# A projection with a 64-row contraction: products of two token tiles in the two row halves of TensorE's array, and a row list read back one block later

## The reference, cut to what matters

```python
scores = jnp.einsum('bsd,d->bs', x, W[0]) + b[0]
_, top_idx = jax.lax.top_k(scores.reshape(B, n_blocks, 128), 16)
h = jnp.take_along_axis(x, sel_idx[:, :, None], axis=1)      # (8, 512, 128)
# retention, on a layer-normalised h
latent = jax.nn.silu(rmsnorm(h, ln_w) @ Wc)                  # 128 -> 64
q, k, v = jnp.split(latent @ Wqkv, 3, axis=-1)               # 64 -> 384
params = (latent @ Wreso).reshape(B, L, H, 4)                # 64 -> 16
gate_val = jax.nn.silu(latent @ Wg)                          # 64 -> 128
...
return out @ Wp * gate_val
```

## Time and profile before

| | |
|---|---|
| median of three runs | 2539.25 us (2531.22 to 2540.06) |
| the profiled execution's own time | 2540.07 us |
| its span, first to last instruction | 2537.9 us |
| busy: TensorE, its weight load, VectorE, ScalarE, GpSimd | 2184.6, 1531.1, 2010.7, 1757.8, 1551.5 us |
| granted TensorE clock, mean of the span | 0.91 |

### The profile page before, as it was taken

One profiled execution on the slowest core, in us unless ns is written; L12 is line 12 of the kernel. 1 busy time (PEld: TensorE's weight loads), 2 busy tenths in 40 slices (PEclk: granted clock), 3 DMA queues, 4 the chain that ended last, 5 costly groups with the idle time before them and its releaser, 6 DMA issues. The chain is left out here.

```text
span 2537.9 us, 48686 instructions
## 1 busy us (share of the span) xinstructions
PE 2184.6 (86%) x12375; PEld 1531.1 (60%) x12376; DVE 2010.7 (79%) x3333; ACT 1757.8 (69%) x5024; POOL 1551.5 (61%) x1693
## 2 busy tenths in 40 slices
PE   4558088683999999999999999999999999966993
PEld 2324066672666666666666666666666666666883
DVE  5943988314999999999999999999999999856664
ACT  2234253251888888888888888888888888823773
POOL 2642812372677777677777776677677767723773
PEclk9855587695999999999999999999999999976997
DMA  6410002351000000000000000000000000034555
GB/s 210 150 26 0 0 1 68 99 150 43 0 1 0 1 0 0 0 0 0 0 0 0 0 0 0 0 0 0 0 0 0 0 0 0 0 77 102 160 152 151
DMA packets 79707, 88.54 MB, mean 35 GB/s; under 512 B 22656, under 2 KB 56448, under 8 KB 77568
## 3 DMA queue, kind: packets, MB, share of 16 engines
q1 hardware_dynamic: 61184, 66.12, 9.3%
q0 software_dynamic: 8192, 16.87, 2.4%
q10 hardware_dynamic: 10240, 4.59, 0.7%
HBM read 73.87 MB, written 13.68 MB: 34 GB/s over the span
## 5 line engine op out<-in xcount | busy, mean ns | idle before, releaser
L1841 POOL TENSOR_TENSOR attend_weights<-attend_weights,attend_scales 128x512 f32<-128x512 f32 x1024 | 1048.5, 1047 | 474.8 <-DVE attend_scales L1757 474.8
L1735 DVE TENSOR_REDUCE attend_maxima<-attend_psL 128x16 fp32r<-128x1024 f32 x512 | 623.8, 1218 | 86.7 <-PE attend_psL L1657 86.7
L1751 DVE TENSOR_REDUCE attend_sums<-attend_weights 128x16 f32<-128x1024 f32 x512 | 618.5, 1208 | 4.1 <-ACT attend_weights L1787 4.1
L1801 ACT ACTIVATE attend_turned<-attend_psT 128x512 f32<-128x512 f32 x1024 | 556.6, 600 | 6.9 <-PE attend_psT L1676 6.6
L1676 PE MATMUL attend_psT<-consts,attend_weights 128*128 128x128 f32 x4096 | 530.4, 272 | 0.9 <-POOL attend_weights L1841 0.9
L1676 PEld LDWEIGHTS attend_psT<-consts,attend_weights 128*128 128x128 f32 x4096 | 477.1, 140 | 69.7 <-POOL attend_weights L1841 3.0
L1689 PE MATMUL attend_psA<-attend_turned,attend_chunk_values 128*64 128x512 f32 x2048 | 495.9, 605 | 0.8 <-ACT attend_turned L1801 0.8
L1795 ACT ACTIVATE attend_weights<-attend_psL,attend_maxima 128x64 f32<-128x64 f32 x2048 | 448.8, 334 | 52.0 <-DVE attend_maxima L1735 52.0
L1656 PE MATMUL attend_psL<-keys,attend_q_high 128*128 (+1 forms) x1024 | 434.2, 424 | 5.6 <-ACT attend_weights L1795 4.0
L1657 PE MATMUL attend_psL<-keys,attend_q_low 128*128 (+1 forms) x1024 | 404.2, 395 | 0.0
L1787 ACT ACTIVATE attend_weights<-attend_psL 128x512 f32<-128x512 f32 x512 | 316.1, 617 | 0.0
(11 more groups left out here) (318 smaller groups left out, 2565.6 us busy)
## 6 DMA issues: line engine op xcount, KB each, us to landing
moe2mix_w_tile<-in_L_ffn_w_dram SPq DMA_DIRECT2D x72, 256.0 KB
select_xbuf<-in_x_dram SPq DMA_DIRECT2D x16, 1024.0 KB, 4.9
moe1mix_w_tile<-in_L_ffn_W_dram SPq DMA_DIRECT2D x40, 256.0 KB, 2.7
select_emb<-L_attn_video_embeds_dram ACTq DMA_DIRECT2D x16, 256.0 KB, 3.1
moe2back_back<-result SPq DMA_DIRECT2D x8, 512.0 KB, 7.2
normed<-moe2route_normed SPq DMA_DIRECT2D x4, 520.0 KB, 9.2
normed<-moe1route_normed SPq DMA_DIRECT2D x4, 512.0 KB, 4.1
moe1back_back<-result SPq DMA_DIRECT2D x4, 512.0 KB, 5.9
```

What stands on the lines that cost most here:

```text
L1735: dve.tensor_reduce(maxima[:, both, :].rearrange("p j v -> p (j v)"), psL[:, both, :].rearrange("p j (v f) -> p (j v) f", f=FR), X, ALU.ma ...
L1751: dve.tensor_reduce(sums[:, both, :].rearrange("p j v -> p (j v)"), weights[:, both, :].rearrange("p j (v f) -> p (j v) f", f=FR), X, ALU. ...
L1801: act.activation(turned[:, parity, :, j * P:(j + 1) * P], psT[:, j % 2, :].rearrange("p (k q) -> p k q", k=SUB), ACT.Copy).then_inc(turned ...
L1841: pool.tensor_tensor(w, w, scales[:, s, :, None].to_broadcast([P, VC, FR]), ALU.mult).then_inc(normalised, 1)
```

## The change

The latents of tokens 0 to 255 of a batch are written to partitions 0 to 63, those of tokens 256 to 511 to partitions 64 to 127: two products of 256 columns, into the two partition halves of `psL`, in place of one of 512, and one silu on 128 partitions. `wall` is loaded a second time, to partitions 64 to 127, by ScalarE's queue. `project` now takes a pair of tiles, one in each row half, in the order q/k/v of half 0, q/k/v of half 1, gate of half 0, gate of half 1, each half with its own PSUM bank; a batch's tiles come in the order 0, 2, 1, 3. GpSimd's `square` therefore waits for the whole batch.

The second row list is written in the selection block but read back in the projection block, between SyncE's loads; GpSimd waits for it after its first two roots. Three small loads have a semaphore of their own (`first_in`), and `between(1)` waits for these alone; the decay rates are made one and two turns of the loop later. The last batch's squares are added up before the first gate step.

```diff
+def get_rows(sp, K, f):
+    part = slice(f * G // 2, (f + 1) * G // 2)
+    sp.wait_ge(K.rows_out, 16 * (f + 1))
+    sp.dma_start(K.rowidx[:, part], K.rows_dram.rearrange("(g p) -> p g", p=P)[:, part],
+                 allow_slow_non_contiguous=True).then_inc(K.rows_back, 16)
...
-        rows = sb("rows", [P, 2, TOP], U32)
+        rows = (sb("rows", [P, TOP], U32), K.last_rows)
...
                 put_rows(1)
-                get_rows(1)
...
-                pool.wait_ge(rows_back, 32)
...
-            wall = sb1("wall", [LAT, QKV + D])
+            wall = sb1("wall", [P, QKV + D])
-            latT = sb1("latT", [LAT, 2, L])
+            latT = sb1("latT", [P, 2, L // 2])
-            psL = ps1("psL", [LAT, L])
+            psL = ps1("psL", [P, 512])
-            psG = ps1("psG", [P, 2, TB, D])
+            psG = ps1("psG", [P, 2, 2, 512])
+            TILES = (0, 2, 1, 3)
+            def load_wall(engine, side):
+                part = slice(side * LAT, (side + 1) * LAT)
+                engine.dma_start(wall[part, 0:3 * D], a["L0_attn_Wqkv"]).then_inc(wall_in, 16)
+                engine.dma_start(wall[part, 3 * D:QKV], a["L0_attn_Wreso"]).then_inc(wall_in, 16)
+                engine.dma_start(wall[part, QKV:QKV + D], a["L0_attn_Wg"]).then_inc(wall_in, 16)
...
             def square(pool, b):
                 for g in range(b * TB, (b + 1) * TB):
-                    pool.wait_ge(qkv_copied, g + 3)
+                    pool.wait_ge(qkv_copied, b * TB + TB + 2)
...
                 def _(sp):
-                    sp.dma_start(wc[:], a["L0_attn_Wc"]).then_inc(s_const, 16)
-                    sp.dma_start(wall[:, 0:3 * D], a["L0_attn_Wqkv"]).then_inc(s_const, 16)
-                    sp.dma_start(wall[:, 3 * D:QKV], a["L0_attn_Wreso"]).then_inc(s_const, 16)
-                    sp.dma_start(wall[:, QKV:QKV + D], a["L0_attn_Wg"]).then_inc(s_const, 16)
+                    sp.dma_start(wc[:], a["L0_attn_Wc"]).then_inc(first_in, 16)
+                    sp.dma_start(lnw[:], column(a["L0_attn_ln_w"])).then_inc(first_in, 16)
+                    sp.dma_start(hd[:], everywhere(a["L0_attn_head_decay"], H0)).then_inc(first_in, 16)
+                    load_wall(sp, 0)
+                    get_rows(sp, K, 1)
                     sp.dma_start(wp[:], a["L0_attn_Wp"]).then_inc(s_const, 16)
-                    sp.dma_start(lnw[:], column(a["L0_attn_ln_w"])).then_inc(s_const, 16)
...
                     sp.dma_start(temp[:], everywhere(a["L0_attn_temperature"], 1)).then_inc(s_const, 16)
-                    sp.dma_start(hd[:], everywhere(a["L0_attn_head_decay"], H0)).then_inc(s_const, 16)
...
                     norm.roots(pool, K, 0, 2)
+                    pool.wait_ge(K.rows_back, 32)
...
                         if b == 1:
-                            dve.wait_ge(s_const, 16 * 11)
+                            dve.wait_ge(first_in, 48)
                             dve.tensor_scalar(wc[:], wc[:], lnw[:, 0:1], None, ALU.mult).then_inc(weights_ready, 1)
-                            dve.tensor_scalar(wp[:], wp[:], memw[:, 0:1], None, ALU.mult).then_inc(weights_ready, 1)
+                        if b == 2:
                             dve.wait_ge(act_decay, 1)
...
-                        if b == 2:
+                        if b == 3:
+                            dve.wait_ge(s_const, 16 * 5)
+                            dve.tensor_scalar(wp[:], wp[:], memw[:, 0:1], None, ALU.mult).then_inc(weights_ready, 1)
                             dve.wait_ge(act_decay, 3)
...
-                    for b in range(B - 3, B - 1):
+                    for b in range(B - 3, B):
                         sum_squares(b)
                     dve.wait_ge(act_gates, 1)
...
-                    sum_squares(B - 1)
...
+                    load_wall(act, 1)
...
                         act.wait_ge(s_latent, b + 1)
-                        act.activation(latT[:, s, :], psL[:], ACT.Silu).then_inc(latent_done, 1)
+                        act.activation(latT[:, s, :], psL[:, 0:L // 2], ACT.Silu).then_inc(latent_done, 1)
...
-                    act.wait_ge(weights_ready, 2)
+                    act.wait_ge(first_in, 48)
...
                         pe.wait_ge(latent_done, b + 1)
-                        pe.matmul(psL[:], wc[:], xnT[:], start=True, stop=True).then_inc(s_latent, 1)
+                        for side in range(2):
+                            mm = pe.matmul(psL[side * LAT:(side + 1) * LAT, 0:L // 2], wc[:], xnT[:, side * (L // 2):(side + 1) * (L // 2)],
+                                           start=True, stop=True, skip_group_check=True)
+                        mm.then_inc(s_latent, 1)
...
-                    def project(b, s, i):
+                    def project(b, s, pair):
...
-                        pe.wait_ge(qkv_copied, b * TB + i + 1)
-                        pe.matmul(psQ[:, i % 2, 0:QKV], lat, wall[:, 0:QKV], start=True, stop=True).then_inc(qkv_ready, 1)
-                        mm = pe.matmul(psG[:, s, i, :], lat, wall[:, QKV:QKV + D], start=True, stop=True, skip_group_check=True)
+                        lat = [latT[side * LAT:(side + 1) * LAT, s, pair * P:(pair + 1) * P] for side in range(2)]
+                        half = [wall[side * LAT:(side + 1) * LAT] for side in range(2)]
+                        for side in range(2):
+                            pe.wait_ge(qkv_copied, b * TB + (2 * pair + side + 1))
+                            pe.matmul(psQ[:, side, 0:QKV], lat[side], half[side][:, 0:QKV], start=True, stop=True).then_inc(qkv_ready, 1)
+                        for side in range(2):
+                            mm = pe.matmul(psG[:, s, side, pair * D:(pair + 1) * D], lat[side], half[side][:, QKV:QKV + D], start=True, stop=True,
+                                           skip_group_check=True)
...
-                    pe.wait_ge(weights_ready, 2)
+                    pe.wait_ge(weights_ready, 1)
                     latent(0)
+                    pe.wait_ge(wall_in, 96)
```

More of the change, by code:

```diff
@@ L137, in __init__ @@
         self.rowidx = sb("rowidx", [P, G], U32)
+        self.last_rows = sb("last_rows", [P, TOP], U32)
+        self.rows_out, self.rows_back = ctx.enter_context(nc.semaphore("rows_out")), ctx.enter_context(nc.semaphore("rows_back"))
         self.consts = sb("consts", [P, CONSTANTS.shape[1]])
@@ L269, in select_and_project @@
         key_highs, key_lows, values_done = sem("key_highs"), sem("key_lows"), sem("values_done")
-        rows_chosen, rows_out, rows_back = sem("rows_chosen"), sem("rows_out"), sem("rows_back")
+        rows_chosen = sem("rows_chosen")
         weights_landed = 16 * (7 + 4 * H1 + 1)
@@ L296, in put_rows @@
                     sp.wait_ge(rows_chosen, f + 1)
[L297 to L303, removed]
+                    sp.dma_start(K.rows_dram.rearrange("(f p r) -> f p r", p=P, r=TOP)[f], rows[f][:]).then_inc(K.rows_out, 16)
                 for c in range(4):
@@ L310, in _ @@
                 load_next(HALF + 4)
-                get_rows(0)
+                get_rows(sp, K, 0)
                 for c in range(HALF + 5, CHUNKS):
@@ L374, in choose @@
                     steps.then(dve.max_index(besti[:, f, 8:16], best[:, f, 8:16], rest[:, f, :]))
-                    dve.tensor_scalar(rows[:, f, :], besti[:, f, :], K.const("blockrow")[:, f:f + 1], None,
+                    dve.tensor_scalar(rows[f][:], besti[:, f, :], K.const("blockrow")[:, f:f + 1], None,
                                       ALU.add).then_inc(rows_chosen, 1)
@@ L458, in _ @@
                         mm.then_inc(values_ready, 1)
-        clear_semaphores(nc, consts_in, rows_back)
+        clear_semaphores(nc, consts_in, rows_chosen)
 def retention(nc, a, K):
@@ L625, in latent, with keep @@
                         act.wait_ge(s_latent, b + 1)
-                        act.activation(latT[:, s, :], psL[:], ACT.Silu).then_inc(latent_done, 1)
-                    def keep(b, i):
+                        act.activation(latT[:, s, :], psL[:, 0:L // 2], ACT.Silu).then_inc(latent_done, 1)
+                    def keep(b, k):
+                        i, side = TILES[k], k % 2
                         g = b * TB + i
-                        act.wait_ge(qkv_ready, g + 1)
+                        act.wait_ge(qkv_ready, b * TB + (k + 1))
                         row = qkv[:, ds(g, 1), :].rearrange("p a d -> p (a d)")
-                        act.activation(row[:, 0:2 * D], psQ[:, i % 2, 0:2 * D], ACT.Copy)
+                        act.activation(row[:, 0:2 * D], psQ[:, side, 0:2 * D], ACT.Copy)
                         act.activation(row[:, 2 * D:].rearrange("p (h e) -> p h e", h=H0)[:, :, 0:DH0],
-                                       psQ[:, i % 2, 2 * D:3 * D].rearrange("p (h e) -> p h e", h=H0), ACT.Copy)
-                        act.activation(params[:, ds(g, 1)].rearrange("p a h c -> p (a h c)"), psQ[:, i % 2, 3 * D:QKV], ACT.Copy).then_inc(qkv_copied, 1)
```

(16 more changed lines are left out.)

9 lines of the change are left out of this document (4 added, 5 removed).

## The result

The changed kernel takes 2495.76 us (median of four runs, 2494.57 to 2496.97), beside 2535.23 for the kernel before in four runs (2531.07 to 2540.06): a ratio of 0.9841, 95% interval 0.9823 to 0.986 (the two medians alone give 0.9844). The sign was right. The likeliest case was not what happened: two of the rivals did, full overlap and the rise of the clock, and behind them GpSimd became the bound.

What follows compares the result with a forecast made beforehand. It took TensorE at 1.2 GHz to bound the projection block, behind a latency-bound front. Its terms, -4.1 - 4.8 - 17.4 - 3.0 - 0.3 = -29.6 us, took 2540.07 to 2510.5, said as 2510; range 2495 to 2532.

Steps and rivals of the forecast that it cites:

- likeliest case: Whole kernel: the forecast of 2510 us, own range 2505 to 2516, chance 0.45.
- full overlap: Pairs in the projection: halves run as two queues, a pair takes 1.76 us, time 2499; rival, chance 0.06.
- rise of the clock: Projection block: TensorE's granted clock rises from 0.50, GpSimd's chain sets the end, -42.9 us, 2497; rival, chance 0.22.
- Selection's end: Selection block's end: with the read-back off its path, the projection begins at 141.0, not 145.1; -4.1 us.
- Projection's start: Head of the projection block: first pair starts 12.2 us into the block, not 17.0; -4.8 us.
- The products: Sixteen tile pairs in the projection: partial overlap in program order, 2.43 us streaming, 1.09 less each; -17.4 us.
- The latents: Projection's latent products: two column halves overlap by one pass, 1.28 us for 1.71; seven in the loop give -3.0 us.
- The read-back "costs nothing, with that cover": Read-back in the projection: GpSimd's 8.5 us per batch stays hidden, rows 2.4, 1.9, 1.1 us ahead in batches 3 to 5.
- The first rival: Projection block: the clock rises and GpSimd's chain sets the end, last copy at 199.8, time 2497; chance 0.22.
- The gates at the end: After the projection's last copy: square root's sine and table load end at 5.75 us, not 6.06; -0.3 us.
- The slower rival: Pairs in the projection: each change of half costs a gap, +5.6 to +16.6 us, 2545 to 2556; chance 0.05.
- the front: Selection's end and projection's start together: earlier block begin, -4.1 us, and earlier first pair, -4.8 us.

Runs made afterwards that it cites:

- e7: Changed kernel with the second row list's read-back and GpSimd's wait for it put back at the selection's end; 2582.0 us, ratio 0.9865 to the kernel before.
- first profile: First profiled execution of the changed kernel itself, last parameter copy at 197.8; median 2495.8 us, ratio 0.9841 to the kernel before.
- e3: Changed kernel with a pair's products ordered wide half 0, gate half 0, wide half 1, gate half 1; 2586.8 us, ratio 0.9866 to the kernel before.
- e4: Changed kernel, products ordered by half, with a wait keeping half 1's products until half 0's have ended; 2615.0 us, ratio 0.9975 to the kernel before.
- e5: Changed kernel with the second half's 16 gathers replaced by plain loads, leaving out those tokens' selection; 2569.4 us, ratio 0.9818 to the kernel before.
- e6: Changed kernel with squares of batches 0 to 2 on VectorE and GpSimd's last roots ahead of its squares; 2568.3 us, ratio 0.9816 to the kernel before.
- e9: Changed kernel run again, unaltered, on another chip beside the kernel before; 2578.0 us, ratio 0.9845 to the kernel before.
- e1: Changed kernel with the old products put back, keeping only the front's changes; 2615.8 us, ratio 0.9958 to the kernel before.

## Why the prediction was right and wrong

**Selection's end: right, undersized.** Said 4.1 us, measured 145.09 - 139.49 = 5.6; in e7, with the wait put back, the block begins 4.5 later than in the first profile. The step that was off took the 2.3 us between landing and next block as the price of any change of block. Without a DMA waited for it is 1.2 us, from 138.3 to 139.49.

**Projection's start: right, undersized.** Said 12.2 us into the block for the first wide product, measured 11.1. Turning at 5.1 (said 5.6), the first latent at 9.0 (said 9.7), and 0.4 more in it since it overlapped fully. The read-back was issued at 3.4 (said 3.2), the first gather at 6.8 (said 8.7 at the latest).

**The products: the failed step.** "I take what the order allows: half 1's first pass of 400 beside half 0's second." e3 and the first profile show that each half keeps an order of its own and does not wait for the other: both wide products start together. A pair is 2.06 us with all its gaps, not 2.73, so the term of 1.09 us a pair is 1.76; a latent with its gap is 1.05, not 1.47. The full-overlap rival had 1.76 without gaps, which is what runs; it was given 0.06 on the ground of program order alone, and no row of before bore that. The sentence of the Trainium skill (TensorE: Matmul & The Clock Gate, Part 3) that products start in program order is not what e3 shows for float32 products in different row halves. The same page's start of such products side by side is (150.9, within 0.05 us), and so, nearly, is the speedup of up to two times that the Trainium skill (TensorEngine Tiling (Array Packing), Overview) gives: a pair fell from 3.82 to 2.06 us, 1.85 times.

**The latents: right in kind.** Column halves overlap as row halves do. In e4, where the row halves don't, the latent still takes 1.05 us.

**The read-back "costs nothing, with that cover": the cover went.** The step weighed GpSimd's 8.5 us against a batch of 7.97 us and found over 1 us of lead. The measured turn is 8.39, but TensorE's batch is 6.2 us at 1.2 GHz (1.04 + 2.06 + 1.05 + 2.06), so the lead is used up by the third batch and TensorE waits 2.5 to 3.5 us in each of three. The first rival did name this chain as the bound, and e5 and e6 bear it out; it gave 50.1 us from the first gather to the last copy, measured were 51.5 and, in e9, 54.4.

**The clock: the rival came about, for the reason given and to little effect.** e4 against e3 shows the reason. The effect was mis-sized: the chain of the first rival does not need the clock, since a batch at 1.2 GHz is shorter than GpSimd's turn. e9 gives one measure of what it is worth: 0.72 in place of 0.87 over the last stretch went with 2.9 us. An estimate for no rise at all: from the turning at 178.97 two batches of 6.2 and the last 11 us give 202.4, 4.6 us later than measured. A kernel with overlap and no rise was not tried. The rule of the Trainium skill (TensorE: Matmul & The Clock Gate, Part 1), that sustained matmul activity releases the throttle, is again not enough: TensorE was busy 98% of 80 us in e4 at 1.2 GHz.

**The gates at the end: right.** Said -0.3 us, measured 10.24 in place of 10.59 from last copy to the next block's first instruction.

**The slower rival** (a gap at each change of half) fell: a pair has 0.30 us beside its 1.76 of streaming, as before.

In sum: 5.6 + 5.95 for the front (said 8.9), 33.1 from the first wide product to the last copy (80.3 before, 47.2 after; said 20.4), 0.35 at the end (said 0.3) and 0.5 later. Full overlap at 1.2 GHz without a wait would have given 16 x 1.76 + 7 x 0.84 = 34.0, where 33.1 were measured: the 9.7 us that TensorE waited for rows and what the clock gave back nearly cancel. That the time still lies inside the range, 0.8 us from its end, is luck in part: neither the full overlap nor the waits were in the forecast.

## What to carry to other kernels

Two independent products with a contraction of 64 rows took the time of one when they were placed in different row halves, here with a PSUM bank each; their order in the program mattered little, but a semaphore wait between them takes all of the overlap away. When a step that bounds a stage is made much shorter, weigh every other engine's turn against the shortest length that the step could have, not the likeliest: here GpSimd's 8.4 us hid behind 10.6 and not behind 6.2, and moving part of its work to a half-idle engine gave another 8 us. Of a load at the head of a block, ask which engine's first long chain hangs on it.

## What the runs showed of the hardware that was not expected

- Two float32 products in different row halves run pass beside pass: 1.49 us for both wide ones at 1.2 GHz, 0.57 for both of 128 columns, in both orders tried (the changed kernel and e3).
- A TensorE busy 98% to 100% of the time for 80 us with one row half at a time stayed at 1.2 GHz (e1, e4, before); with both at once, in the first profile, the first pair began at 150.55, the granted clock was 0.50 in 152 to 153, 0.59 in the next microsecond and 1.00 from 154 on, and it was at 0.50 again around or right behind each of the three long waits for rows.
- The block is the same program in each execution, but ended 3.8 us apart in two of them: 0.9 by when the first gather was issued, 2.9 in the stretch in which the clock stood at 0.72 and not 0.87.
